# A 64-channel cross attention inside a twelve-stage decoder kernel: its scores in three products of rounded parts instead of one full-precision product

## The reference

```python
q = (query @ Wq + bq).reshape(b, s, 16, 64)
k = (key @ Wk + bk).reshape(b, key.shape[1], 16, 64)
v = (value @ Wv + bv).reshape(b, value.shape[1], 16, 64)
logits = jnp.einsum('bshd,bShd->bhsS', q, k) / np.sqrt(64)
weights = jax.nn.softmax(logits, axis=-1)
attn = jnp.einsum('bhsS,bShd->bshd', weights, v).reshape(b, s, 1024)
return attn @ Wo + bo
...
x = _layernorm(x + that, axis=-1)
```

## Time and profile before

| | us |
|---|---|
| runs | 2590.77, 2596.3, 2597.23 |
| median | 2596.3 |
| profiled execution, first to last instruction (its span) | 2588.6 |
| its own time is not listed apart; the run nearest above its span | 2590.77 |
| the stage, from its first multiplication at 609.2 to the last step of its norm at 954.9 | about 346 |
| slots: from maxima(0) at 626.92 to maxima(63) at 942.43 | 315.5 |

### The profile page before, as it was taken

One profiled execution on the slowest core, in us unless ns is written; L12 is line 12 of the kernel. 1 busy time (PEld: TensorE's weight loads), 2 busy tenths in 40 slices (PEclk: granted clock), 3 DMA queues, 4 the chain that ended last, 5 costly groups with the idle time before them and its releaser, 6 DMA issues. The chain is left out here.

```text
span 2588.6 us, 42273 instructions
## 1 busy us (share of the span) xinstructions
PE 2152.8 (83%) x14834; PEld 1675.5 (65%) x14834; DVE 1553.4 (60%) x3631; ACT 1120.6 (43%) x3143; POOL 582.1 (22%) x725
## 2 busy tenths in 40 slices
PE   6799674668999986869978869979996899798994
PEld 4566432226777754549956537869995566598884
DVE  4566648995555562456565454545554555656996
ACT  5566344452444433443311443433332356454662
POOL 0200017992000010010022320000002322133555
PEclk9899787899999986669987979979997899797997
DMA  3000012120000003314310004422210000155772
GB/s 112 9 2 2 33 67 78 63 64 33 1 1 1 1 32 109 102 63 163 137 42 0 5 7 130 110 79 91 93 62 27 13 6 6 51 166 169 242 245 85
DMA packets 58247, 174.92 MB, mean 68 GB/s; under 512 B 18327, under 2 KB 28155, under 8 KB 56008
## 3 DMA queue, kind: packets, MB, share of 16 engines
q1 hardware_dynamic: 56012, 169.23, 20.1%
q0 software_dynamic: 2048, 3.29, 0.4%
HBM read 154.11 MB, written 18.38 MB: 67 GB/s over the span
## 5 line engine op out<-in xcount | busy, mean ns | idle before, releaser
L2410 PE MATMUL ps<-l1a_zc,tables_sb 128*128 128x400 f32 x256 | 109.2, 560 | 95.2 <-POOL l1a_zc L2339 59.2
L2410 PEld LDWEIGHTS ps<-l1a_zc,tables_sb 128*128 128x128 f32 x256 | 47.7, 204 | 156.6 <-POOL l1a_zc L2339 87.5
L1912 ACT ACTIVATE l1x_probs<-ps,l1x_nmax 100x361 f32<-100x361 f32 x128 | 70.8, 558 | 164.3 <-DVE l1x_nmax L1987 164.3
L2350 POOL TENSOR_TENSOR l1a_dbx<-l1a_dx,l1a_rows 128x400 f32<-128x400 f32 x128 | 130.4, 1054 | 7.2 <-DMA l1a_rows<-l1a_rows_spilled 5.2
L2363 ACT ACTIVATE ps<-l1a_delta,weights 128x400 f32<-128x400 f32 x128 | 76.5, 598 | 81.5 <-DVE ps L2393 53.5
L3025 PE MATMUL ps<-l3f_routed_x_high,l3f_routed_w_low 128*128 128x128 f32 x320 | 92.7, 290 | 15.7 <-DVE l3f_routed_w_low L3089 14.2
L1026 ACT ACTIVATE l3x_probs<-l3x_s_sb,l3x_nmax 100x361 f32<-100x361 f32 x128 | 75.2, 589 | 69.8 <-DVE l3x_nmax L1115 65.8
L1024 ACT ACTIVATE l0x_probs<-ps,l0x_nmax 100x361 f32<-100x361 f32 x128 | 70.8, 558 | 64.7 <-DVE l0x_nmax L1122 56.5
L2602 PE MATMUL ps<-l2f_x_high,l2f_w_high 128*128 128x400 f32 x272 | 95.2, 350 | 0.0
L2393 DVE TENSOR_TENSOR_SCAN ps<-ps,l1a_dbx 128x400 f32<-128x400 f32 x86 | 84.6, 994 | 17.0 <-POOL l1a_dbx L2350 10.1
L2601 PE MATMUL ps<-l2f_x_high,l2f_w_low 128*128 128x400 f32 x272 | 94.7, 348 | 0.0
(11 more groups left out here) (714 smaller groups left out, 6737.1 us busy)
## 6 DMA issues: line engine op xcount, KB each, us to landing
ctxT<-l_ffn_units SPq DMA_DIRECT2D x20, 1026.0 KB, 5.5
l3f_expert<-l_ffn_units SPq DMA_DIRECT2D x20, 1026.0 KB, 5.7
l2x_a_taps<-l2x_taps_spread SPq DMA_DIRECT2D x8, 1912.5 KB
l2f_landing<-l_ffn_units SPq DMA_DIRECT2D x17, 771.0 KB, 4.4
l1a_rows<-l1a_rows_spilled SPq DMA_DIRECT2D x32, 400.0 KB, 3.4
l1f_gates<-l1f_gates SPq DMA_DIRECT2D x16, 800.0 KB, 4.2
l1f_positions<-l1f_staged SPq DMA_DIRECT2D x16, 621.9 KB
l1f_landing<-l_ffn_units SPq DMA_DIRECT2D x16, 512.0 KB, 3.5
```

The lines of the kernel that those rows point to most:

```text
L2350: pool.tensor_tensor(dbx[:, n % BUFS, :], dx[:, j, m, :], rows[:, g % RING, 0, :], ALU.mult).then_inc(s.dbx_ready, 1)
L2410: pe.matmul(y_bank(m), st.ident, zc[:, n % DONE, :], start=(i == 0), stop=(i == NS - 1)).then_inc(s.sum_done, 1)
```

## The change

Scores of a pair are now made from rounded parts (`fp32r`, one pass of the array per product): q_high·k_high + q_high·k_low + q_low·k_high, six products per pair, three for each head, 362 columns wide (the reach of the tile is one column more, which is filled once from a constant). `kT` becomes `kT_high` and `kT_low`, with a ring of three pairs in place of four. Key copy: ACT writes `kT_high` (rounded), then DVE writes `kT_low` = projection + bias - `kT_high`, and the side bank is free only after that (`k_split`). Query copy: DVE writes the full sum to one buffer `q_sum`, ACT rounds it to `q_high`, POOL writes `q_low` = `q_sum` - `q_high`; the next query copy on DVE waits for that.

```diff
-    K_RING = 4
+    QK = KEYS + 1
+    K_RING = 3
...
                 elif kind == "k":
-                    pe.wait_ge(s.k_copied, n + 1)
+                    pe.wait_ge(s.k_split, n + 1)
...
                 for j in range(B):
                     pool.tensor_tensor(norm.resid[:, j, :], x_b(j), bias_rows[:], ALU.add).then_inc(s.x_biased, 1)
+                def split_queries(n):
+                    jj, g = divmod(n, PER_HALF)
+                    pool.wait_ge(s.q_cut, n + 1)
+                    pool.tensor_tensor(r(q_low[:, 2 * g:2 * g + 2].rearrange("p m b t -> p (m b t)")), q_sum[:],
+                                       q_high[:, 2 * g:2 * g + 2].rearrange("p m b t -> p (m b t)"), ALU.subtract).then_inc(s.q_split, 1)
+
+                for n in range(PER_HALF):
+                    split_queries(n)
                 for j in range(B):
+                    ahead = PER_HALF * (j // 2 + 1) if j % 2 == 0 and j // 2 + 1 < B // 2 else None
+                    if ahead:
+                        split_queries(ahead)
+                        split_queries(ahead + 1)
                     rstd_pool(pool, norm, s, j)
+                    if ahead:
+                        split_queries(ahead + 2)
+                        split_queries(ahead + 3)
...
-                    pe.wait_ge(s.k_copied, p + 1)
-                    pe.wait_ge(s.q_copied, PER_HALF * (j // 2) + m // 2 + 1)
+                    pe.wait_ge(s.k_split, p + 1)
+                    pe.wait_ge(s.q_split, PER_HALF * (j // 2) + m // 2 + 1)
...
                     for i in range(2):
                         group = slice(HD * i, HD * (i + 1))
-                        last = pe.matmul(pair_tile[:, i, :], qT[group, m, j % 2, :], kT[group, p % K_RING, :], start=True, stop=True, tile_position=(HD * i, 0))
+                        pe.matmul(score_tile[:, i, :], r(q_high[group, m, j % 2, :]), r(kT_high[group, p % K_RING, :]), start=True, stop=False, tile_position=(HD * i, 0))
+                    for i in range(2):
+                        group = slice(HD * i, HD * (i + 1))
+                        pe.matmul(score_tile[:, i, :], r(q_high[group, m, j % 2, :]), r(kT_low[group, p % K_RING, :]), start=False, stop=False, tile_position=(HD * i, 0))
+                    for i in range(2):
+                        group = slice(HD * i, HD * (i + 1))
+                        last = pe.matmul(score_tile[:, i, :], r(q_low[group, m, j % 2, :]), r(kT_high[group, p % K_RING, :]), start=False, stop=True, tile_position=(HD * i, 0))
...
-                        act.activation(kT[:, n % K_RING, :], st.ps[:, bank, 0:KEYS], ACT.Identity, bias=bias["k"][:, m:m + 1]).then_inc(s.k_copied, 1)
+                        act.activation(r(kT_high[:, n % K_RING, 0:KEYS]), st.ps[:, bank, 0:KEYS], ACT.Identity, bias=bias["k"][:, m:m + 1]).then_inc(s.k_copied, 1)
+                    elif kind == "q":
+                        i = PER_HALF * n + part
+                        act.wait_ge(s.q_copied, i + 1)
...
+                        act.activation(r(q_high[:, 2 * part:2 * part + 2].rearrange("p m b t -> p (m b t)")), q_sum[:], ACT.Copy).then_inc(s.q_cut, 1)
...
                     if kind == "q":
                         dve.wait_ge(s.q_ready, PER_HALF * n + part + 1)
...
+                        if PER_HALF * n + part >= 1:
+                            dve.wait_ge(s.q_split, PER_HALF * n + part)
...
+                    elif kind == "k":
+                        j, m = divmod(n, PAIRS)
+                        dve.wait_ge(s.k_copied, n + 1)
+                        if n >= K_RING:
+                            dve.wait_ge(s.scores_ready, n - K_RING + 1)
+                        dve.scalar_tensor_tensor(r(kT_low[:, n % K_RING, 0:KEYS]), st.ps[:, bank, 0:KEYS], bias["k"][:, m:m + 1], kT_high[:, n % K_RING, 0:KEYS],
+                                                 ALU.add, ALU.subtract).then_inc(s.k_split, 1)
...
                     if p < pairs:
                         maxima(p)
+                    for x in items[p][0]:
+                        copy_out(x)
                     if 0 <= p - 2 < pairs:
                         copy_turned(p - 2)
```

More of the change, by code:

```diff
@@ L1731, in wide_heads @@
         norm = all_batches(nc, ctx, st, f"{name}_heads")
-        qT = sb("qT", [P, PAIRS, 2, S])
-        kT = sb("kT", [P, K_RING, KEYS])
+        q_sum = sb("q_sum", [P, 4 * S])
+        q_high, q_low = sb("q_high", [P, PAIRS, 2, S]), sb("q_low", [P, PAIRS, 2, S])
+        kT_high, kT_low = sb("kT_high", [P, K_RING, KEYS + 1]), sb("kT_low", [P, K_RING, KEYS + 1])
         vals = sb("vals", [KROWS, 2, T, VW])
@@ L1744, in wide_heads @@
         r = lambda ap: ap.bitcast(F32R)
-        sems = ["probs_set", "bias_made", "bias_ready", "x_biased", "q_ready", "q_copied", "k_ready", "k_copied", "v_ready", "v_copied",
+        sems = ["probs_set", "bias_made", "bias_ready", "x_biased", "q_ready", "q_copied", "q_cut", "q_split", "k_ready", "k_copied", "k_split", "kT_spare_set", "v_ready", "v_copied",
                 "scores_ready", "max_ready", "exp_done", "turned", "even_copied", "odd_copied", "values_done", "o_copied",
@@ L1751, in wide_heads @@
             pair_tile = st.ps[0:S, 0:2, 0:KEYS]
+            score_tile = st.ps[0:S, 0:2, 0:QK]
             turned_tile = lambda i: st.ps[0:KROWS, T_BANK + i, 0:T * S]
@@ L1775, in _ @@
                 pool.memset(probs[:], 0.0).then_inc(s.probs_set, 1)
+                pool.tensor_copy(r(kT_high[:, :, KEYS]), st.head_mask[64][:, 0:1].to_broadcast([P, K_RING])).then_inc(s.kT_spare_set, 1)
+                pool.tensor_copy(r(kT_low[:, :, KEYS]), st.head_mask[64][:, 0:1].to_broadcast([P, K_RING])).then_inc(s.kT_spare_set, 1)
                 pool.wait_ge(s.bias_ready, 1)
@@ L1833, in scores @@
                     j, m = divmod(p, PAIRS)
-                    pe.wait_ge(s.k_copied, p + 1)
-                    pe.wait_ge(s.q_copied, PER_HALF * (j // 2) + m // 2 + 1)
+                    pe.wait_ge(s.k_split, p + 1)
+                    pe.wait_ge(s.q_split, PER_HALF * (j // 2) + m // 2 + 1)
+                    if p == 0:
+                        pe.wait_ge(s.kT_spare_set, 2)
                     if p == 0:
@@ L1896, in copy_out @@
                             act.wait_ge(s.scores_ready, n - K_RING + 1)
-                        act.activation(kT[:, n % K_RING, :], st.ps[:, bank, 0:KEYS], ACT.Identity, bias=bias["k"][:, m:m + 1]).then_inc(s.k_copied, 1)
+                        act.activation(r(kT_high[:, n % K_RING, 0:KEYS]), st.ps[:, bank, 0:KEYS], ACT.Identity, bias=bias["k"][:, m:m + 1]).then_inc(s.k_copied, 1)
+                    elif kind == "q":
+                        i = PER_HALF * n + part
+                        act.wait_ge(s.q_copied, i + 1)
+                        if n > 0:
+                            act.wait_ge(s.scores_ready, PAIRS * (2 * n - 1) + 2 * part + 2)
+                        act.activation(r(q_high[:, 2 * part:2 * part + 2].rearrange("p m b t -> p (m b t)")), q_sum[:], ACT.Copy).then_inc(s.q_cut, 1)
                     elif kind == "turn_x":
@@ L1964, in copy_out @@
                         dve.wait_ge(s.q_ready, PER_HALF * n + part + 1)
-                        if n > 0:
-                            dve.wait_ge(s.scores_ready, PAIRS * (2 * n - 1) + 2 * part + 2)
-                        dve.scalar_tensor_tensor(qT[:, 2 * part:2 * part + 2, :, :].rearrange("p m b t -> p m (b t)"),
+                        if PER_HALF * n + part >= 1:
+                            dve.wait_ge(s.q_split, PER_HALF * n + part)
+                        dve.scalar_tensor_tensor(q_sum[:].rearrange("p (m t) -> p m t", m=2),
                                                  st.ps[:, bank, 0:4 * S].rearrange("p (m t) -> p m t", m=2), 0.125,
```

## The result

The changed kernel takes 2608.2 us in the median (2604.27 to 2610.71, six runs), against 2593.53 of the kernel before in six runs. The ratio is 1.006, with a 95% interval of 1.0043 to 1.0078, which is +11 to +20 us. The forecast was 2611 against a median of 2596.3, +15.0 us; measured are +14.7. Later runs (`low_late`, `front_first`, `one_product`, `all_three`) stand beside 22 of the kernel before with a median of 2592.36, of which one slow run, 3573.13 us at a granted clock of 0.54, is left out of every ratio.

What follows compares the result with a forecast made beforehand. PE bounds the kernel before; after the change a DVE and ACT chain sets the slots. Front 8.5, first eight slots 4.4, sixteens 2.1, last eight 0 sum to +15.0 us: 2611 us median, own range 2604 to 2622, whole range 2600 to 2627.

Steps and rivals of the forecast that it cites:

- scores on PE, per slot: Six one-pass products per pair on PE take 0.66 us against 0.79, saving 0.12 per slot; bounds 0.50 and 1.10.
- kT_low to the next instruction: DVE's added kT_low instruction, in 62 slots, counts 0.45 us; bounds 0.39 and 0.57.
- chain in a bare slot: DVE's wait to 2.64, then kT_low, turned copy, reciprocal and two scalings: 4.31 us before the next maxima can start.
- each sixteen: Sixteen slots of full work: 84.3 us against 83.60, +0.7; DVE alone 82.6, PE alone 81.7.
- front: Stage's start: query sums wait for POOL's order and the single buffer, +6.8, plus 1.7 for slow clock: +8.5 us (6.8 to 10.4).
- The waits between PE and DVE in the heavy slots: PE and DVE wait for each other around query and output slots: +0.9, +0.2, +0.5 and +0.1 us per sixteen.
- Costed at nothing: ACT's 12 more query roundings, POOL's 12 other subtractions, the ring of three and two column fills were taken to add no time.
- A: Row halves do not overlap for rounded parts: scores take 1.10 us, PE bounds again, 2626 us; chance 0.10.
- B: PE stays the bound, kT_low starting by 1.5 us: 18 us saved less 6.8 at the front, 2585; chance 0.08.
- C: DVE's chain is cheaper, 0.06 us less per slot, with the front at its low end: 2599 to 2603; chance 0.10.
- D: PE, waiting in light slots, falls to the lower clock; four value slots cost 15 us: 2626; chance 0.08.
- the marks given: Signs: maxima(0) near 635.5; slots 36.7 and 84.3 us; DVE idle about 107 us; PE idle before its turn; scores 0.66.

Runs made afterwards that it cites:

- low_late: Changed kernel with DVE's kT_low of pair p+2 moved from behind maxima(p) to behind scale(p-1): 2594.43 us, ratio 1.0007 to the kernel before.
- front_first: Changed kernel with POOL's four query subtractions at the stage's start put ahead of its eight additions: 2609.53 us, ratio 1.0056 to the kernel before.
- one_product: Changed kernel with scores from q_high·k_high only, the two products with low parts left out: 2618.97 us in a single run.
- all_three: Changed kernel with kT_low behind scale, POOL's subtractions before its additions, and separate places for the first four query sums: 2587.05 us, ratio 0.9974 to the kernel before.
- wait alone: Kernel before with one added DVE wait, behind maxima(p), for ACT's key copy of pair p+2, without work: 2599.47 us.
- work alone: Kernel before with one added DVE instruction like kT_low behind maxima(p), on keys long there, so without a wait: 2590.6 us.
- ring of three: Kernel before with three places for keys instead of four: 2595.56 us in a single run.
- wait and work: Kernel before with both the added DVE wait for the key copy of pair p+2 and the added instruction behind it: 2607.57 us.

## Why the prediction was right, step by step

| step | forecast | measured |
|---|---|---|
| scores on PE, per slot | 0.66 us | 0.66 |
| start of kT_low after the maxima | 2.64 | 2.62 |
| kT_low to the next instruction | 0.45 | 0.51 |
| chain in a bare slot | 4.31 | 4.34 |
| first eight slots | +4.4 | +4.6 |
| each sixteen | 84.3 | 84.46 to 84.50 |
| three groups of sixteen | +2.1 | +2.5 |
| last eight slots | 0 | +0.35 |
| front | +8.5 | +7.2 |
| total in the stage | +15.0 | +14.6 |

The slots came out 0.9 us longer than forecast and the front 1.3 shorter, and these nearly cancel in the total.

- **The bound moves from PE to a chain of DVE and ACT.** Right, and shown from both sides: with `kT_low` behind the scaling the slots fall to 81.9, with only a third of the score products they stay at 83.3, where PE as the bound would have given 79.2. That it takes the wait and the work together was in the sum (a wait to 2.64 and 0.45 of work against PE's 4.55 in a value slot) but not said; the three runs on the kernel before show it.
- **kT_low** was under-sized. It lasts 0.594 us, longer than the query copy of 400 columns (0.575) and the row that I took (0.531); 0.51 from start to start, inside the bounds. A hand-over shorter by 0.02 and shorter steps behind it took half of that back.
- **The waits between PE and DVE in the heavy slots** were 1.7 us per sixteen in the forecast. By the links as measured, the chain alone gives 83.1 per sixteen (0.03 more in each slot), so they were 1.4.
- **The front** was over-sized by 1.3. The rounds came as forecast (sums end at 624.6, 627.0 and 629.4, with a stage that starts 1.0 later). The clock did fall, from 623.7 to 630.5, to the lower of its levels: 0.57 in the mean from 623 to 631 (windows below). But it fell under the key items, which wait for the sums anyway, and only the first two value products ran slow, so that 1.7 were counted where some 0.5 arose. What the difference is taken against is chance as well: the front of the kernel before takes 17.7 us in three profiles (before, wait alone, work alone), each with a fall of the clock at its start, and 16.25 in two without one (ring of three, wait and work). Against these two the changed front would be +8.6 us.

```profile
610.00:623.00 13.00, 10.69 (x48) 9.04 (x48) 6.36 (x7) 5.13 (x6) 8.97 (x14) 0.87 0.44 159
623.00:631.00 8.00, 5.92 (x17) 4.68 (x18) 2.29 (x5) 2.51 (x5) 4.00 (x4) 0.57 0.00 0
```

- **Costed at nothing:** the ring of three, shown; ACT's roundings and POOL's subtractions in the slots cost little if anything, as the slots keep 6.8 us of some 8 saved on PE with both in place; no run takes them out.
- **The rivals:** A falls with the 0.66. That 0.66 is hit so closely is in part luck: it was chosen between 0.50 and 1.10, and no row before the change had such products on row halves. B (PE stays the bound) needed `kT_low` to start earlier; moving it behind the scaling instead gave B's regime, with a scores saving of 0.12 where B had 0.29. C, a cheaper chain, falls (its lower end comes to 2598 by its own terms, not 2599). D happened in a small way: the clock fell once in the first eight slots of the changed kernel (0.95), where PE had time to spare, and cost nothing there: with POOL's order changed the same slots take 36.91 us at 1.00. D's price was added up wrongly, 4 x (9.1 - 4.92) being 16.7 and not 15, and its reading of the earlier trace rows does not hold: the stretch at 0.89 has PE busy all the time, 16.00 of 16 us, and the next one, which was not among the rows, is at 1.00 with PE busy 93%:

```profile
626.00:660.00 34.00, 31.73 (x216) 22.79 (x216) 21.19 (x43) 16.26 (x48) 0.00 (x0) 1.00 0.00 1
```

- **Of the marks given,** one did not hold: PE idle ahead of its turn, ended by the scaling, shows only 4.5 us. The chain holds PE up mostly at another place, ahead of the scores, which wait for the exps of the pair before: the 8.1 us between 660 and 943 that stand in the waits after. And a busy share under 99% was a weak mark, 97.5% being so near.

The rule cited of the Trainium skill (FP8 and Floating Point Precision, TensorE Precision Notes: four passes for true FP32, so three quarters with three) would have put the scores at 0.59 us; the trace shows 0.66, in starts 0.24, 0.17 and 0.25 apart.

## What to carry to other kernels

An in-order engine that takes part of a split copy waits for its partner's whole queue: place the second half where the first is already done, behind the work that needs nothing new, and the same instruction is free. A wait that hides in the slack and a piece of work that hides in the slack can each cost next to nothing and together set the pace, so sum the chain through both engines for each kind of slot and compare it with the bound engine's slot, not the busy shares. A saving on the bound engine is worth what the next chain leaves of it: here 0.12 us in each of 63 slots turned into a loss of 7.4 us, and into a gain of 6.8 by moving two lines.

## What was not expected of the hardware

PE's clock falls at single places among the slots: at 661.3 us in the changed kernel, at 679.9 with POOL's order changed, at 641.6 and 846.4 with one product, and again at 955.6 at the end of that stage. In these three kernels the chain of DVE and ACT sets the pace and PE waits for it. Each of the five falls comes within 1.2 us after PE has stood 1.5 us ahead of the scores, waiting for ACT's exps. In the changed kernel:

```profile
660.11 0.41 PE L1864 MATMUL ps<-l1x_kT_high,l1x_q_high 64*100 64x362 f32 x2 [1.50 <-ACT l1x_probs L1946]
```

Such a pause is not enough: of twelve of them in the ten profiles seven were followed by no such fall, two of these in the wait and work together, where the clock never falls in the slots. In the six profiles in which PE's slots set the pace (the kernel before, `kT_low` behind the scaling, all three mended, the wait alone, the work alone, the ring of three) PE never stands longer than 1.21 us in the slots, and the clock does not fall there either. What decides it beyond that was not tried, and no run changes the pauses alone. Two falls cost time in the slots, 1.3 us at 679.9 and 0.7 at 846.4; two, in the light slots, cost none; the one at 955.6 made the end of the stage 5.1 us longer. So an engine just off the critical path may run slower when it is needed next.
